# Attention, routing and experts of a decoder layer in one block, with twelve expert tiles run among the last routing steps

## The reference, cut to what matters

```python
x = x + _L0_attn_ref(_layernorm(x), ...)            # recurrent mixer, x is (32, 100, 256)
x = x + _L0_xattn_ref(_layernorm(x), ctx_768, ...)  # 16 heads over 361 keys
x = x + _L0_ffn_ref(_layernorm(x), Wr, W1, W2)
# _L0_ffn_ref: N = 3200 tokens, E = 8 experts, K = 2, F = 512
logits = flat @ Wr.T
weights, ids = jax.lax.top_k(logits, K)
weights = jax.nn.softmax(weights, axis=-1)
h = jnp.einsum('nc,efc->nef', flat, W1)
val, gate = (h[..., :F], h[..., F:])
act = val * jax.nn.silu(gate)
expert_outputs = jnp.einsum('nec,ne->nc', einsum('nef,ecf->nec', act, W2), router_weights)
```

## Time and profile before

| | us |
|---|---|
| median of 3 runs | 1555.5 (1554.47 to 1556.44) |
| the profiled execution's own time | 1543.22 |
| span of the profiled execution | 1541.4 |
| PE busy | 1337.4 |
| DVE busy | 992.6 |
| POOL busy | 798.2 |
| ACT busy | 576.4 |

### The profile page before, as it was taken

How to read it: one execution, slowest core, us unless ns; L and a number is a source line. 1 busy time by engine, 2 the same in 40 slices (tenths; PEclk the granted TensorE clock), 3 DMA queues, 4 the chain that set the end, 5 groups by cost and what they waited for, 6 DMA issues and landing times. The chain is left out here.

```text
span 1541.4 us, 31333 instructions
## 1 busy us (share of the span) xinstructions
PE 1337.4 (87%) x9914; PEld 898.5 (58%) x9915; DVE 992.6 (64%) x2041; ACT 576.4 (37%) x1420; POOL 798.2 (52%) x1138
## 2 busy tenths in 40 slices
PE   4787788778863899999999999999983999999996
PEld 2465455456552566666666666666652566666664
DVE  2687977977872378888888888888882222222221
ACT  1334233233320355555555555555541221212221
POOL 3235623633533567777777777777763222222222
PEclk9999999999976699999999999999995999999999
DMA  4995000000001554545455555555431223222231
GB/s 144 278 294 155 0 1 1 0 0 0 1 1 33 96 101 105 126 121 125 120 126 122 126 123 122 126 124 124 118 84 42 45 43 46 44 44 45 43 48 21
DMA packets 152681, 127.99 MB, mean 83 GB/s; under 512 B 41363, under 2 KB 145443, under 8 KB 152547
## 3 DMA queue, kind: packets, MB, share of 16 engines
q1 hardware_dynamic: 140242, 112.22, 29.7%
q0 software_dynamic: 12304, 14.10, 6.0%
HBM read 36.10 MB, written 44.83 MB: 53 GB/s over the span
## 5 line engine op out<-in xcount | busy, mean ns | idle before, releaser
L1365 DVE TENSOR_REDUCE neg_raw<-bank_s 100x2 f32<-100x722 f32 x256 | 229.0, 895 | 22.9 <-PE bank_s L1558 22.7
L1899 POOL DMA_INDIRECT out<-result,target x57 | 88.2, 1547 | 267.1 <-DVE result L1873 264.0
L1239 ACT ACTIVATE prob<-bank_st 120x400 f32<-120x400 f32 (+1 forms) x384 | 166.2, 514 | 152.2 <-PE bank_st L1577 152.2
L1376 DVE TENSOR_SCALAR bank_st<-bank_st 121x1200 f32<-121x1200 f32 x128 | 180.4, 1409 | 1.4 <-PE bank_st L1568 0.6
L751 PE MATMUL bank_l<-q_heads,k 128*100 128x192 f32 (+4 forms) x512 | 124.1, 383 | 63.9 <-DVE attn L565 51.0
L1884 DVE TENSOR_TENSOR hidden<-silu,ebank_v 128x512 f32<-128x512 f32 x57 | 39.2, 687 | 197.0 <-PE ebank_v L1808 197.0
L751 PEld LDWEIGHTS bank_l<-q_heads,k 128*100 128x100 f32 x512 | 81.4, 177 | 114.0 <-DVE attn L565 43.5
L399 ACT ACTIVATE q_heads<-q 32x192 f32<-32x192 f32 (+3 forms) x168 | 62.1, 369 | 226.1 <-DVE q L524 217.7
L1094 POOL TENSOR_TENSOR neg_diag<-xident_b,neg_max 100x400 bf16<-100x400 bf16 x128 | 109.1, 853 | 35.2 <-DVE neg_max L1370 34.6
L1558 PE MATMUL bank_s<-k_st,q_st 96*128 96x361 bf16 x512 | 123.2, 322 | 3.8 <-DVE neg_raw L1365 2.4
L1568 PE MATMUL bank_st<-q_st,k_st 96*128 96x100 bf16 x1536 | 112.8, 209 | 5.7 <-ACT prob L1239 0.6
(11 more groups left out here) (207 smaller groups left out, 2737.8 us busy)
## 6 DMA issues: line engine op xcount, KB each, us to landing
k_st<-k_part SPq DMA_DIRECT2D x384, 90.2 KB
slot_rows<-empty SPq DMA_DIRECT2D x9, 2967.0 KB, 28.8
q_st<-q_part SPq DMA_DIRECT2D x192, 50.0 KB
kv<-in_ctx_t SPq DMA_DIRECT2D x32, 270.8 KB
expert_w<-in_w SPq DMA_DIRECT2D x16, 512.0 KB, 4.4
rows<-slot_rows SPq DMA_DIRECT2D x57, 129.0 KB, 2.0
residual<-in_w SPq DMA_DIRECT2D x16, 256.0 KB, 4.3
residual<-in_x SPq DMA_DIRECT2D x8, 400.0 KB
```

Source lines behind the costliest of these rows:

```text
L1239: act.activation(prob[0:KEYS[c], t % 2, c], bank_st[0:KEYS[c], c, 0:4 * T], ACT.Exp).then_inc(exp_done, 1)
L1365: dve.tensor_reduce(neg_raw[:, h:h + 2], bank_s[0:T, :, 0:S], AX.X, ALU.max, negate=True).then_inc(max_done, 1)
L1376: dve.tensor_scalar(tile, tile, CLAMP, -CLAMP, ALU.min, ALU.max).then_inc(clipped, 1)
```

## The change

The two blocks of attention and of experts become one. A second map of tiles is made early: at step t = 2 of the last batch PE sums the counts of the first 14 pairs of batches (`total_before`), and DVE lists twelve full tiles of those counts (`first_map`, 14 steps; a tile counts if at least 128 rows of its expert stand). SP loads them as soon as that map is done. The stages of tiles 0 to 3 are written by hand into the last routing steps on PE, ACT and DVE, tiles 4 to 11 follow, and the remaining 45 tiles are listed by a later map (`used_map` of 4 steps in batch 31, then `rest_ends` of 6, `rest_experts` of 4 and `rest_rows` of 4, put between stages of tiles 3, 4 and 5). The adds of tiles 0 and 1 stand on POOL ahead of the last `route_pair`, the rest behind the last `send`s. Expert stages use banks of PSUM that the last attention step has left, and their buffers lie where the stacks of batches 29 and 30 and `kv` lay. `first` is now called `rows_turn`, `out` `expert_out`. The number of tiles is still 57.

```diff
+FIRST = 12
+assert 2 * (BATCH * T - 4 * T) // 2 - 7 * 127 >= 128 * FIRST
...
     with ExitStack() as ctx:
...
+        used = sb("used", [1, E])
+        used_rows = sb("used_rows", [1, E + 1])
+        cap_used = sb("cap_used", [1, E])
+        row_base = sb("row_base", [1, TILES])
+        q_st, k_st = [None] * 3, [None] * 3
+        q_st[1] = sb("q_st1", [96, NH * T + Q_OVER], BF16)
+        k_st[1] = sb("k_st1", [96, NH * S + K_OVER], BF16)
+        with ExitStack() as dead:
+            for place in (2, 0):
+                k_st[place] = dead.enter_context(nc.sbuf_tensor(f"k_st{place}", [96, NH * S + K_OVER], BF16))
+                q_st[place] = dead.enter_context(nc.sbuf_tensor(f"q_st{place}", [96, NH * T + Q_OVER], BF16))
+            kv = dead.enter_context(nc.sbuf_tensor("kv", [KC, 2, 2, S], F32))
...
+        FIRST_MAP = 14
+        ALL_MAP = FIRST_MAP + 4 + 6 + 4 + 4
...
+        ebank_v = (bank_st[:, 0], bank_st[:, 1])
+        ebank_g = (bank_st[:, 2], bank_s[:, 0])
+        ebank_x, ebank_y, ebank_h = bank_s[:, 1], bank_v, bank_o
...
+        def later_tiles(eng, body):
+
+            with eng.Fori(FIRST // R, TILES // R) as k:
+                for i in range(R):
+                    body(R * k + i, i % R, i % 2)
+            for i in range(TILES - TILES % R, TILES):
+                body(i, i % R, i % 2)
...
             keep(BATCH - 2)
             load_w2(BATCH // 2 - 2)
+
+            def row_tile(i, r):
+                at = sp.value_load(tile_row[0:1, bass.ds(i, 1)], min_val=0, max_val=SLOTS - 128)
+                until(result_done, i - R + 1)
+                until(loaded, 16 * i)
+                sp.dma_start(rows[:, r], slot_rows[bass.ds(at, 128), :]).then_inc(loaded, 16)
+
+            until(step, FIRST_MAP)
+            for hp in range(2):
+                until(scattered[hp], SENT * (BATCH // 4 - 1))
+            for i in range(R):
+                row_tile(i, i)
             keep(BATCH - 1)
             load_w2(BATCH // 2 - 1)
+            for i in range(R, FIRST):
+                row_tile(i, i % R)
+            until(step, ALL_MAP)
+            for hp in range(2):
+                until(scattered[hp], SENT * BATCH // 4)
+            later_tiles(sp, lambda i, r, bank: row_tile(i, r))
             until(out_stored, 16 * BATCH)
 
         @block.gpsimd
...
+            def add(i, r):
+                pool.wait_ge(target_done, i + 1)
+                pool.wait_ge(result_done, i + 1)
+                after(pool, added, 16 * i)
+                pool.sem_inc(pool_waited, 1)
+                pool.indirect_dma_start(
+                    out=out, out_offset=bass.IndirectOffsetOnAxis(ap=target[:, r:r + 1], axis=0),
+                    in_=result[:, r % U], in_offset=None, compute_op=ALU.add).then_inc(added, 16)
+
             last = BATCH // 2 - 1
...
             norm3(BATCH - 1)
+            pool.wait_ge(out_stored, 16 * (BATCH - 1))
+            add(0, 0)
+            add(1, 1)
             route_pair(last)
             tag(last, 1)
             for j in range(2):
                 for c in range(2):
                     send(last, 1, j, c)
-            for hp in range(2):
-                pool.wait_ge(scattered[hp], SENT * (last + 1) // 2)
+            pool.wait_ge(out_stored, 16 * BATCH)
+            for i in range(2, FIRST):
+                add(i, i % R)
+            later_tiles(pool, lambda i, r, bank: add(i, r))
+            pool.wait_ge(added, 16 * TILES)
...
             out_copy(BATCH - 1)
             turned3(BATCH - 2, bank_v)
             second_row(BATCH - 2, 2)
+            silus(0, 0, 0)
+            hidden_turn(0, 0)
             heads_turn(BATCH - 1)
+            silus(1, 1, 1)
+            hidden_turn(1, 1)
             norm3(BATCH - 1, 3, BATCH // 4 - 1)
+            silus(2, 2, 0)
             turned3(BATCH - 1)
             second_row(BATCH - 1, 3)
+            hidden_turn(2, 2)
+            silus(3, 0, 1)
             gap_exps(BATCH // 2 - 1)
+            hidden_turn(3, 0)
+            for i in range(4, FIRST):
+                expert_tile(i, i % R, i % 2)
+            later_tiles(act, expert_tile)
 
         @block.vector
...
+            def first_map():
+                seen = E - 1
+                over = past[:, 0:FIRST, 0:seen]
                 dve.wait_ge(totalled, 1)
-                then(dve.tensor_copy(n_rows[:], bank_v[0:1, 0:E]))
-                then(dve.tensor_tensor(needs, n_rows[:].unsqueeze(2).to_broadcast([1, E, EXPERT_TILES]),
+                then(dve.tensor_scalar(n_rows[:], bank_m[0:1, 256:256 + E], -127.0, None, ALU.add))
+                then(dve.tensor_tensor(needs(seen), n_rows[:, 0:seen].unsqueeze(2).to_broadcast([1, seen, EXPERT_TILES]),
+                                       iota_full[:].unsqueeze(1).to_broadcast([1, seen, EXPERT_TILES]), ALU.is_gt))
+                then(dve.tensor_reduce(n_tiles[:, 0:seen], needs(seen), AX.X, ALU.add))
+                then(dve.tensor_tensor_scan(end_tile[:, 0:seen], ones[0:1, 0:seen], n_tiles[:, 0:seen], 0.0, ALU.mult,
+                                            ALU.add))
+                then(dve.tensor_scalar(skip[:, 0:seen], n_tiles[:, 0:seen], -128.0, float(CAP), ALU.mult, ALU.add))
+                then(dve.tensor_tensor(over, iota_tile[:, 0:FIRST].unsqueeze(2).to_broadcast([1, FIRST, seen]),
+                                       end_tile[:, 0:seen].unsqueeze(1).to_broadcast([1, FIRST, seen]), ALU.is_ge))
+                then(dve.tensor_reduce(expert_f[:, 0:FIRST], over, AX.X, ALU.add))
+                then(dve.tensor_copy(tile_expert[:, 0:FIRST], expert_f[:, 0:FIRST]))
+                then(dve.tensor_tensor(over, over, skip[:, 0:seen].unsqueeze(1).to_broadcast([1, FIRST, seen]),
+                                       ALU.mult))
+                then(dve.tensor_reduce(row_f[:, 0:FIRST], over, AX.X, ALU.add))
+                then(dve.scalar_tensor_tensor(row_f[:, 0:FIRST], iota_tile[:, 0:FIRST], 128.0, row_f[:, 0:FIRST],
+                                              ALU.mult, ALU.add))
+                then(dve.tensor_copy(tile_row[:, 0:FIRST], row_f[:, 0:FIRST]))
+                then(dve.tensor_tensor(used[:, 0:seen], end_tile[:, 0:seen], n_tiles[:, 0:seen], ALU.subtract))
+                then(dve.tensor_scalar(end_tile[:, 0:seen], end_tile[:, 0:seen], float(FIRST), None, ALU.min))
+                assert steps[0] == FIRST_MAP
...
+                    if t == 2 and not more:
+                        first_map()
+                    if t == 3 and not more:
+                        used_map()
...
             last = BATCH // 2 - 1
+            rows_turn(0, 0)
             place(last - 1, 0)
+            gated(0, 0, 0)
             normalise(BATCH - 1)
             best_two(BATCH - 2, 0, last, bank_v)
+            rows_turn(1, 1)
+            gated(1, 1, 1)
             residual(BATCH - 1, (BATCH - 1) % 2)
             moments3(BATCH - 1)
+            rows_turn(2, 2)
+            result_out(0, 0)
+            gated(2, 2, 0)
+            rows_turn(3, 3)
+            result_out(1, 1)
             best_two(BATCH - 1, 1, last)
             one_hots(last)
+            gated(3, 0, 1)
             place(last, 1)
-            tile_map()
+            rest_ends()
+            rows_turn(4, 4)
+            result_out(2, 2)
+            gated(4, 1, 0)
+            rest_experts()
+            rows_turn(5, 5)
+            result_out(3, 3)
+            gated(5, 2, 1)
+            rest_rows()
+            rows_turn(6, 0)
+            result_out(4, 4)
+            for i in range(6, FIRST):
+                expert_tile(i, i % R, i % 2)
+            later_tiles(dve, expert_tile)
...
+                    if not more and t == 2:
+                        pe.wait_ge(earlier_next, BATCH // 2 - 2)
+                        pe.wait_ge(x_done, BATCH - 1)
+                        total_before(earlier[:, 0])
...
+            pe.wait_ge(max_done, 2 * 4 * BATCH)
+            rows_turn(0, 0)
+            pe.wait_ge(step, FIRST_MAP)
+            pe.wait_ge(w1_loaded, 16 * 2 * E)
+            weigh(BATCH - 1, (BATCH - 1) % 2, 3)
+            turn3(BATCH - 2, 2, v_done, 3 * BATCH, bank_v)
+            count(last - 1, x_done, BATCH - 1)
+            up(0, 0, 0)
+            back_turn(BATCH - 1, chosen_done, last)
+            route(BATCH - 2, bank_v)
+            rows_turn(1, 1)
+            down(0, 0)
+            out_turn(BATCH - 1)
+            up(1, 1, 1)
+            out_project(BATCH - 1)
+            rows_turn(2, 2)
+            pe.wait_ge(index_done, BATCH - 1)
+            pe.wait_ge(w2_loaded, 16 * (2 * E - 1))
+            expert_out(0, 0)
+            down(1, 1)
+            up(2, 2, 0)
+            turn3(BATCH - 1, 3, x_done, BATCH)
+            rows_turn(3, 3)
+            expert_out(1, 1)
+            route(BATCH - 1)
+            down(2, 2)
+            up(3, 0, 1)
+            pe.wait_ge(earlier_done, last + 1)
+            pe.wait_ge(index_done, BATCH)
+            total(earlier[:, 1], pairs[:, 1])
```

(38 more changed lines are left out.)

295 lines of the change are left out of this document (104 added, 191 removed).

## The result

The changed kernel takes 1533.76 us (median of 4 runs, 1531.24 to 1535.0), the kernel before beside it 1555.53 (1554.47 to 1556.44): a ratio of 0.9858, with a 95% interval of 0.9841 to 0.9875, 21.8 us less. The forecast was 1533.5.

A forecast was written before the change was run, and what follows sets the result against it. PE alone bounds the expert stage; at the seam it waits and its clock falls. Tile 6 moving from 1228.55 to 1206.1 saves 22.4 us, less 0.3 for memsets: 22 off 1555.5 gives 1533.5 us, range 1527 to 1542.

The forecast's parts named there:

- Part A: From the early map to first rows on PE: `first_map` 3.4 us, shift at 1158.2, rows on PE at 1160.0.
- Part B: Low-clock stretch at tile 0: its `up` starts at 1163.4 and ends at 1169.0, between 1168.0 and 1170.0.
- Part C: From tile 0's `up` to tile 6: 33.6 us of PE work plus 3.5 of waits, tile 6 at 1206.1.
- restarts behind late waits: Between tile 0's `up` and tile 6: four late waits restart PE at 0.3 us each, 1.2 in all.
- The sum: Whole kernel: tile 6 comes 22.4 us earlier, less 0.3 for memsets: 22 us off, 1533.5 from 1555.5.
- Table loads: ACT in the woven stretch: three loads of 1.28 us instead of one; the two more are hidden and cost nothing.
- 1: Woven stretch: clock stays at 1.2 GHz through part of it, losing 8 to 18 us, 1542 to 1552; chance 0.09.
- 2: Woven stretch and on: clock low through tile 11, a loss of 35 us, 1590; chance 0.04.
- 3: POOL ahead of `route_pair`: adds hold back routing, PE waits at `total`; 3 to 8 us, 1537 to 1541; chance 0.10.
- 4: Seam of the blocks: no overlap, only the block's end saved, some 9 us, 1546; chance 0.03.

The follow-up runs named there:

- e10: Changed kernel with the last batch's attention ended before tile 0, clip before `first_map`, other map parts behind the row copies, all adds late: 1529.86 us, 0.9857 of before.
- e11: Changed kernel with the edits of e9 and e10 together: 1529.35 us, 0.9855 of before.
- e5: Changed kernel once more, no edit, on chip B: 1533.15 us beside 1553.62 for the kernel before, 0.9872.
- e6: Changed kernel with DVE's copies of rows for tiles 4 to 6 ahead of the later map's pieces: 1532.04 us, 0.9849 of before.
- e4: Changed kernel with all adds on POOL behind the last scatters, none ahead of `route_pair`, on chip A: 1518.92 us, 0.9846 of before.
- e7: Changed kernel with two more exponents between ACT's silus, so four more table loads, seven in all: 1533.15 us, 0.9864 of before.
- e3: Changed kernel with six early tiles instead of twelve, on chip A: 1528.71 us, 0.9907 of before.
- e2: Changed kernel with early map and row loads but no tile stages woven into the routing, all adds late, on chip A: 1529.08 us, 0.992 of before.
- e12: Changed kernel with two scatters around the fourth diagonal multiply, two around the next batch's first `route_pair` piece, adds late, row copies early: 1528.39 us, 0.9847 of before.
- e8: Changed kernel with each pair's second scatter behind the fourth diagonal multiply, the fourth behind the next batch's first: 1538.59 us, 0.9905 of before.
- e1: Kernel before once more, no edit, on chip A: 1539.87 us in its one run, 1542.31 as median of seven beside the group.
- e9: Changed kernel with another POOL operation between any two scatters, so none adjoin: 1531.98 us, 0.9863 of before.

## Why the prediction was right

**Part A.** `first_map` was put at 3.4 us and takes 4.0 (1163.44 to 1167.44): the scan over seven elements took 0.81, where 0.16 had been counted. That is no cost of the scan. It starts 0.07 us after POOL's diagonal multiply (1164.28 to 1165.13) and ends 0.03 after it, in all ten profiles that have this order; in e10 and e11, where that multiply is over before the scan begins, the same scan takes 0.16. The shift, put at 1158.2, is at 1169.00, which is 1158.8 after the 10.2 are off; the rows, put on PE at 1160.0 (1156.6 + 3.1 would be 1159.7), are there at 1160.6. The row loads that stand ahead of the last batch's store on SP cost nothing, as argued.

**Part B.** `up` of tile 0 was to start at 1163.4 and starts at 1163.3; it was to end at 1169.0, between 1168.0 and 1170.0, and ends at 1169.7, which is what the prediction gave for the low level throughout. The clock did rise under it, but only 5.5 us in, 0.9 before its end; the rise that the prediction took over from the kernel before, at 1165.6, did not come. When it rises differs between executions of the same kernel: in e5 it is 2.5 us into this `up`, which takes 4.94 us there and 6.41 here.

**Part C.** 33.6 us of work and 3.5 of waits were put between that end and tile 6, 37.1 in all. Measured from 1179.93 to 1216.06 it is 36.1, of which PE is busy 34.0 and idle 2.15. The waits before tiles 4 to 6, put at 1.5 us, are 2.0 by e6. Before tile 1 0.66 stands for 0.8. Nothing is left for the 1.2 us of restarts behind late waits. PE does not wait at `total`. So tile 6 came at 1205.9 for 1206.1, and that it is this close is luck in part: B ends 0.7 late and C is 1.0 short.

**The sum** of 22 us holds (21.8 in the medians, 20.5 in e5, 23.4 in e4, which has its adds late as well). But the step from the profiled execution to the median, 12.3 us "for a reason that no row shows", was right only as a difference: it is the pace of attention. The profiled execution of before took 39.56 us a pair and 1543.2 in all, as chip A does (39.58, 1542.31); its runs took what chips B, C and D take. The execution of after ran at the slower pace, which is why it did not come out at 1521 but at 1531.24: 1521 and the 10.2 of attention. That the timed runs of before ran at that slower pace is argued from their times; no profile of before on such a chip was taken. That the timed runs of after met the slower pace too was luck: beside 1542.31 on chip A, e4 took 1518.92, under the whole stated range of 1527 to 1542.

**Table loads.** ACT's two more loads were put at nothing against a rule of the Trainium skill (ScalarE: Activation LUTs, "Rules for kernel authors": finish all calls of one table set before switching, and budget about 2.7 us a switch). The trace has 1.28 us for each of the three, and e7 with seven shows no loss in the median. In this stretch, where ACT is busy 6.66 and 4.87 of 20 us, the rule costs nothing to break that the median shows, and the measurement decides.

**Rivals.** 1 and 2, the clock low in the woven stretch: it is 1.00 from 1180 on; only in e3, with its wait of 5.97 us, is it lost once more. 3, POOL's adds hold back the routing: the order is as feared and only 0.09 us lay between POOL's sum and PE's count, for the 1 us foreseen, but it sufficed. In e4, with the adds moved away, the sum is there 1.7 us ahead of the count (1184.39 and 1186.12), and nothing is gained. 4, only the block's end is saved: e2 shows how much comes without weaving, 13 us, more than the 9 put down for it, since the early map brings the rows too.

## What to carry to other kernels

Weave the first independent pieces of the next stage into the last dependent chain of this one, and give the next stage enough pieces to cover that chain's landing and planning too: six tiles left a wait of 6 us and a clock at half, twelve none. Judge such a change by the distance between two events around it (here the shift and tile 6), not by spans: two executions of the same attention code stood 10 us apart before the change's place was reached. And an edit that frees one wait must be followed to the next waiter on the engine it shifts: the scatters set apart took 8.9 us of PE's waits away (5.7 and 3.6 down to 0.4) and made 10.3; the late adds were harmless alone and undid the early copies in e12, though not in e10, where the routing ends earlier.

## What the runs showed of the hardware that was not expected

The same kernel takes 1542.31 us on one chip and 1551.8 to 1553.62 on three others, in every run (ranges of 1540.6 to 1545.36 and 1549.5 to 1558.05). At the slower pace a maximum on DVE that is due while POOL issues the second of two adjoining scatters starts 0.3 to 0.8 us after the end of that scatter (after, e5 to e8, e10); at the faster one it starts during it (before, e1 to e4). A scatter with no other beside it holds none at either pace: in e8 the maximum starts 0.7 us into it. In e9, where at least 1.4 us lie between scatters, none was held, but few fell due within one.

The maxima read PSUM. The Trainium skill (SBUF — State Buffer, "Who interferes with whom") has it that a DVE instruction with at most one SBUF input, outside certain modes of DVE, does not contend with GpSimd. These rows show one that is held, on chips B and C, and not on A. What holds it, and why not on A, stays open: no run here took the scatters out or gave them another issuer.

A scan over seven elements on DVE takes 0.81 us when POOL's diagonal multiply has begun 0.07 us before it (ten profiles), and 0.16 when that multiply is over (e10, e11). A scatter does not do this: in e10 a scan at 1197.64 lies wholly within one (1197.56 to 1198.55) and takes 0.16.

The moment at which the clock rises differs between executions of one kernel: 5.5 us into tile 0's `up` in one and 2.5 in another (after, e5), so that it took 6.41 and 4.94 us, which moves all behind it by 1.5 us. By the Trainium skill (TensorE: Matmul & The Clock Gate, "What you observe") the transition varies by 0.5 us either way from run to run; it varies here too, but by 3 us.
